# A fused attention and expert kernel: a ring of 27 results, expert shares on ScalarE, a dense layer in place

## What is computed

```python
xn = layernorm(x)
q, k, v = heads(xn @ Wq), heads(xn @ Wk), heads(xn @ Wv)          # 16 heads of 16
k_c, v_c = blocks_of_16(k) @ Wck, blocks_of_16(v) @ Wcv           # 32 blocks
logits_c = where(block_is_past, q @ k_c / 4, -1e9)
out_c = softmax(logits_c) @ v_c                                   # compressed blocks
top_idx = top_k(logits_c, 4)                                      # four blocks of each token
out_s = softmax(q @ k[tokens of top_idx] / 4) @ v[...]            # selected blocks
out_l = softmax(q @ k / 4 within the last 32 tokens) @ v          # local window
attn = (g0 * out_c + g1 * out_s + g2 * out_l) @ Wo
# expert layer: 4 heads, two sets of 64 keys, the best 8 of all pair sums
sx, sy = top_k(sim_x, 8), top_k(sim_y, 8)
scores, pk = top_k(sx[:, None] + sy[None, :], 8)
w = silu(xn . down_embed[idx]) * softmax(scores)
experts = sum(w * up_embed[idx])
mlp = (silu(xn @ Wg + bg) * (xn @ Wu + bu)) @ Wd + bd
out = x + attn + mlp + experts
```

## Time and profile before

| | |
|---|---|
| median of 3 executions | 1988.92 us (1987.8 to 1990.62) |
| the profiled execution | 1987.12 us, its span 1985.3 us |
| TensorE matmul busy | 1642.0 us, 83% |
| TensorE weight load busy | 1191.8 us, 60% |
| VectorE busy | 1366.6 us, 69% |
| ScalarE busy | 839.5 us, 42% |
| GpSimd busy | 918.3 us, 46% |
| granted TensorE clock, mean | 0.919 |
| stretch before the turns (0 to 262 us) | TensorE 208.21 us busy |
| stretch of the turns (262 to 1932 us) | TensorE 1396.57, VectorE 1252.15, ScalarE 731.27, GpSimd 819.15 us busy |
| stretch behind them (1932 to 1986 us) | TensorE 37.21 us busy |

### The profile page before, as it was taken

The page is one execution under the profiler, slowest core; times in us unless marked ns, Lnnn a source line. Parts: engine busy times, 40 slices in busy tenths (PEclk is TensorE's granted clock), DMA queues, the critical chain, the costliest instruction groups (busy, mean ns, idle before and its releaser), DMA issues. The chain is left out here.

```text
span 1985.3 us, 43216 instructions
## 1 busy us (share of the span) xinstructions
PE 1642.0 (83%) x14480; PEld 1191.8 (60%) x14480; DVE 1366.6 (69%) x4732; ACT 839.5 (42%) x1520; POOL 918.3 (46%) x741
## 2 busy tenths in 40 slices
PE   4999768888888888888888888888888888888867
PEld 3777636655555566666555655666565555566656
DVE  4344277777777777777777777777777777777742
ACT  0655234444344444444444444444444344444431
POOL 4533254455454554545555444454445545454420
PEclk7999878999899999998999899998999899999988
DMA  5455401111111101111111011111111111101017
GB/s 175 161 168 167 151 20 35 34 33 33 33 33 33 30 25 33 33 33 33 33 31 28 25 33 32 29 33 33 33 33 33 33 33 33 33 23 33 13 32 240
DMA packets 151611, 105.11 MB, mean 53 GB/s; under 512 B 63336, under 2 KB 145688, under 8 KB 151576
## 3 DMA queue, kind: packets, MB, share of 16 engines
q1 hardware_dynamic: 143128, 96.27, 16.5%
q10 hardware_dynamic: 8448, 8.39, 1.3%
HBM read 64.45 MB, written 40.16 MB: 53 GB/s over the span
## 5 line engine op out<-in xcount | busy, mean ns | idle before, releaser
L1076 POOL TENSOR_TENSOR cw<-cw,mw 128x1024 f32<-128x1024 f32 x96 | 226.7, 2362 | 368.0 <-DVE mw L1353 368.0
L1261 DVE TENSOR_REDUCE bmax<-q_bank 128x32 f32<-128x512 f32 (+3 forms) x512 | 227.0, 486 | 123.7 <-PE q_bank L1482 123.7
L1062 POOL TENSOR_TENSOR sumxy<-xy 128x1024 f32<-128x1024 f32 x128 | 240.8, 1903 | 0.0
L1137 ACT ACTIVATE pts<-k_bank 128x512 f32<-128x512 f32 (+2 forms) x384 | 185.0, 491 | 115.9 <-PE k_bank L1518 112.9
L1630 PE MATMUL y_bank<-wfd,hT 128*128 128x256 f32 x512 | 146.9, 412 | 76.5 <-DVE hT L1252 76.5
L1482 PE MATMUL q_bank<-ko,qo 96*128 96x512 bf16 (+3 forms) x512 | 144.6, 309 | 50.4 <-DVE bmax L1261 50.2
L1285 DVE TENSOR_REDUCE lmax<-q_bank 128x8 f32<-128x512 f32 x64 | 44.2, 691 | 196.9 <-PE q_bank L1504 196.9
L1047 POOL TENSOR_TENSOR shift_s<-unsel,smax_hi 128x496 bf16<-128x496 bf16 x32 | 32.6, 1017 | 310.3 <-DVE smax_hi L1300 310.3
L1464 PE MATMUL f_bank<-xt,wfg 128*128 128x128 f32 x1024 | 163.5, 289 | 0.0
L1464 PE MATMUL f_bank<-xt,wfu 128*128 128x128 f32 x1024 | 158.8, 277 | 0.0
L1630 PEld LDWEIGHTS y_bank<-wfd,hT 128*128 128x128 f32 x512 | 96.4, 204 | 100.0 <-DVE hT L1252 82.5
(11 more groups left out here) (231 smaller groups left out, 3751.2 us busy)
## 6 DMA issues: line engine op xcount, KB each, us to landing
qo<-s_qs SPq DMA_DIRECT2D x192, 64.0 KB, 2.2
ko<-s_ks SPq DMA_DIRECT2D x192, 64.0 KB, 2.2
s_qs<-parts SPq DMA_DIRECT2D x8, 768.0 KB, 3.8
s_ks<-parts SPq DMA_DIRECT2D x8, 768.0 KB, 6.2
s_v<-vo SPq DMA_DIRECT2D x8, 544.0 KB, 3.0
vv<-s_v SPq DMA_DIRECT2D x32, 136.0 KB, 2.3
xin<-in_L_attn_x_dram SPq DMA_DIRECT2D x8, 512.0 KB, 6.7
s_xt<-xT SPq DMA_DIRECT2D x8, 512.0 KB, 6.9
```

The lines of the kernel that those rows point to most:

```text
L1062: done("sum_done", g_.tensor_tensor(sumxy[:, h, :, :], xy[:, 0, h, 0:XK, None].broadcast_to([P, XK, KEYS]), xy[:, 1, h, None, :].broadcast ...
L1076: done("cw_sum", g_.tensor_tensor(cw[:, :], cw[:, :], mw[:, h % 2, :], ALU.add))
L1137: last = s.activation(pts[:, h, OFFS[j]:OFFS[j] + n], bank[:, 0:n], ACT.Exp)
L1261: last = v.tensor_reduce(bmax[:, i, h, 0:n], Q.bank(job)[:, o:o + n * BLK].rearrange("p (n j) -> p n j", j=BLK), AX.X, ALU.max)
```

## The change

**Ring K.** `pcT` is now the first result, `aug` and `co` share one bank as `augco`, and there are 27 results. On TensorE `block_shares` (the pcT transposes) stands between w0 and w1; `shifts_and_blocks` (aug and co) stands behind sim; `before_windows` (off) keeps its place among the rows of g0. Co no longer stands behind a0.

**Expert weights.** VectorE's two operations a head become one scalar_tensor_tensor, which also sums its row; ScalarE multiplies each row by 1/sum of the softmax (`share`); GpSimd adds the four rows. The reduction over cw goes: four sums, times erec, added. The last two operations of `last_expert` move to GpSimd.

**Dense layer.** tanh, gate and up work in hT itself; tanh of w0 and w1 in sw. `mlp_down` waits for u0 before its first part and for u1 before its third.

**Order.** On VectorE expert 3 moves ahead of the gate, `best_blocks` behind the experts, match_replace in two halves of eight into head 1's maxima, `best_keys` behind gate 1, `block_shares` ahead of the pair sums, and the shifts behind `normalize(t, 0)`. On GpSimd and ScalarE the order changes as shown.

```diff
-            k_jobs = ["aug", "pcT", "off", "a0", "co"]
+            k_jobs = ["pcT", "augco", "off", "a0"]
...
 # GpSimd
                     for h in range(PH):
                         done("sum_done", g_.tensor_tensor(sumxy[:, h, :, :], ...
-                        if h == 0:
+                        if h == 1:
+                            if now:
+                                silu_weights(now)
                             need(pool, "c8_done", t)
                             done("e8_in", g_.tensor_tensor(e8[:, :, :], ...
-                            if behind:
-                                silu_weights(behind)
+                def last_expert(t):
+                    need(pool, "csm_done", t)
+                    need(pool, "cw_sum", t)
+                    done("clast_sum", g_.tensor_tensor(clast[:, :], cw[:, EX - 1:EX], csum4[:, :], ALU.subtract))
+                    need(pool, "clast_sum", t)
+                    done("clast_done", g_.tensor_tensor(cw[:, EX - 1:EX], clast[:, :], four[:, :], ALU.add))
+                def weights(t, heads):
+                    for h in heads:
+                        need(pool, "ms_done", t, h + 1)
                         if h > 1:
                             need(pool, "cw_sum", t, h - 1)
+                        done("cw_sum", g_.tensor_tensor(cw[:, :], mw[:, 0, :] if h == 1 else cw[:, :], mw[:, h, :], ALU.add))
...
                 def step(t):
-                    weights(t)
+                    weights(t, (1,))
                     if n:
                         compressed(n)
-                    if n:
-                        candidates(n, behind=t)
+                    weights(t, (2, 3))
+                    last_expert(t)
+                    if n:
+                        selection(n, now=t)      # strike, pc_in
+                        candidates(n, now=t)
+                        result_in(t)
+                        block_shares(n)
+                        shifts(n)
...
 # ScalarE
+                def share(t, h):
+                    need(act, "mw_done", t, h + 1)
+                    done("ms_done", s.activation(mw[:, h, :], mw[:, h, :], ACT.Copy, scale=erec[:, h:h + 1]))
...
                 def step(t):
-                    tanh(t, "w0", tw[:, 0, :], "tw_done")
+                    tanh(t, "w0", sw[:, 0:512], "tw_done")
+                    block_shares(t)
                     expert(t, 0)
-                    tanh(t, "w1", tw[:, 1, :], "tw_done")
+                    tanh(t, "w1", sw[:, 512:EX], "tw_done")
                     expert(t, 1)
-                    shifts(t)
+                    share(t, 0)
+                    expert(t, 2)
                     if n:
                         key_scores(n)
+                    share(t, 1)
+                    shifts_and_blocks(t)
+                    expert(t, 3)
                     openings(t)              # off, a0, tanh of g0
+                    share(t, 2)
+                    share(t, 3)
                     head(t, 0)
                     head(t, 1)
-                    tanh(t, "g1", th[:, 1, :], "th_done")
+                    tanh(t, "g1", hidden(1), "th_done")
+                    if n:
+                        pc_exp(n)
                     head(t, 2)
                     if n:
                         e8_exp(n)
                     head(t, 3)
...
 # VectorE
                 def expert(t, h):
-                    cf.link(v.tensor_scalar(dst, sumxy[:, h, :, :]..., c8[:, h, 7:8], erec[:, h:h + 1], ALU.is_ge, ALU.mult))
+                    need(dve, "sum_done", t, h + 1)
                     need(dve, "ex_done", t, h + 1)
-                    done("mw_done", v.tensor_tensor(dst, dst, ex[:, h % 2, :], ALU.mult))
+                    done("mw_done", v.scalar_tensor_tensor(mw[:, h, :], sumxy[:, h, :, :]..., c8[:, h, 7:8],
+                                                           ex[:, h % 2, :], ALU.is_ge, ALU.mult, accum_out=csm[:, h:h + 1]))
...
                 def step(t):
                     expert(t, 2)
+                    expert(t, 3)
+                    expert_sum(t)
+                    if n:
+                        best_blocks(n)
                     gate(t, 0)
                     # maxima of head 0
                     up(t, 0)
-                    expert(t, 3)
+                    # selection(n, (0, 1)), maxima of head 1, selection(n, (2, 3))
                     gate(t, 1)
+                    # block_max(n, 2, 0), best_keys(n), block_max(n, 2, 1), block_max(n, 2, 2)
-                    last_expert(t)
                     up(t, 1)
+                    # unselected, best_pairs, maxima of head 3, block_shares, pair_sums, local_max(n, 0)
+                    normalize(t, 0)
+                    # local_max(n, 1), selected_max(n)
                     result(t)
-                    normalize(t, 0)
                     normalize(t, 1)
...
 # TensorE
                 def mlp_down(t, part):
                     if part == 0:
                         Y.wait_free(pe, t, "y")
-                        F.wait_read(pe, t, "u1")
+                    if part % 2 == 0:
+                        F.wait_read(pe, t, f"u{part // 2}")
...
                     token_rows(t, "w0", wdn, 0)
+                    block_shares(t)
                     token_rows(t, "w1", wdn, 512)
                     if n:
                         compressed(n)
-                    openings(t, 0)
-                    if n:
                         token_rows(n, "sim", wsim, 0)
                         loaded_by(pe, parts_in, N_PARTS, n)
-                    openings(t, 1)
+                    shifts_and_blocks(t)
                     up_rows(t, "g", 0, 0)
                     up_rows(t, "g", 0, 1)
-                    openings(t, 2)
+                    before_windows(t)
                     up_rows(t, "g", 0, 2)
                     head_shifts(t, 0)
                     up_rows(t, "g", 0, 3)
-                    openings(t, 3)
```

More of the change, by code:

```diff
@@ L1037, in compressed, with selection @@
                                                      block_no[:, :, None, :].broadcast_to([P, TT, HG, NB]), ALU.add))
-                def shifts(t):
+                def selection(t, now=None):
                     need(pool, "top_done", t)
@@ L1050, in shifts, with candidates @@
                         ALU.add))
[L1051 to L1055, removed]
+                def candidates(t, now=None):
                     need(pool, "xy_in", t)
@@ L1182, in openings @@
                 def openings(t):
-                    K.wait_full(act, t, "pcT")
-                    K.released("pcT", s.activation(pcT[:, :], K.bank("pcT")[:, :], ACT.Copy))
-                    expert(t, 2)
                     K.wait_full(act, t, "off")
@@ L1418, in step @@
                     up(t, 0)
-                    expert(t, 3)
                     if n:
+                        selection(n, (0, 1))
                         for part in range(3):
                             block_max(n, 1, part)
-                        best_keys(n)
+                        selection(n, (2, 3))
                     gate(t, 1)
@@ new lines, in before_windows @@
+                def before_windows(t):
+                    bank = K.bank("off")
+                    K.wait_free(pe, t, "off")
+                    K.wait_read(pe, t, "augco")
+                    mm(bank[96:128, 0:384], identb[:, 96:128], window_off[:, None, :].broadcast_to([P, 12, 32]),
+                       start=True, stop=True)
+                    for h in range(HG):
+                        for i in range(TT - 1):
+                            o = 32 * ((TT - 1) * h + i)
+                            tq = slice(P * (i + 1), P * (i + 1) + 32)
+                            mm(bank[96:128, o:o + 32], ko[0:SP3, t.half, h, P * i + 96:P * i + P], qo[0:SP3, t.half, h, tq],
+                               start=False, stop=False, skip_group_check=True)
+                            last = mm(bank[96:128, o:o + 32], headones[:, h, 0:32], shiftT[:, tq], start=False,
+                                      stop=True, skip_group_check=True)
+                    K.filled("off", last)
```

213 lines of the change are left out of this document (109 added, 104 removed).

## The result

The changed kernel takes 2008.71 us (median of 4 runs, 2007.99 to 2010.49); the kernel before, run beside it, 1989.18 (4 runs, 1987.8 to 1990.62). The ratio is 1.0099, 95% interval 1.0082 to 1.0117: slower by about 1%. The profiled execution took 2007.99 us with a span of 2006.1, so the span grew by 20.8.

The account below looks back on a forecast made before the run. A chain over several engines was taken to set each turn, 52.06 us before and 52.5 after. 31 x 0.44 = 13.6, less 4.8, made 1987.12 into 1995.9, plus 1.8 for the median: 1998 us, range 1945 to 2060.

Parts of the forecast that it names:

- tanh g0 (1) and (2): From w0 through ScalarE's row of work to off at 10.2, then 2.58 to tanh g0 at 12.75 us.
- strike done (3): GpSimd's cw sums of heads 2 and 3, 2.35 each, then four small operations including strike: done at 20.15 us.
- xy (4): VectorE's match_replace, head 1's maxima, gate 1 and best_keys, handing over to GpSimd's xy at 29.15 us.
- e8_in done (5): GpSimd's xy and cand, two sumxy, silu 2.35 and e8_in 0.24: done at 37.3 us.
- d3 (6): ScalarE's e8, then s30's exponentials: d3 starts at 38.05 us, after TensorE idles 5.6.
- Steps 7 and 8: d3 to the next w0, 11.72 us at full clock, plus 2.7 for half clock after the idle: 52.5 a turn.
- 31 x 0.44 = 13.6, less 4.8: Sum over turns: 31 turns each 0.44 us longer, the last turn 4.8 shorter, +8.8 us in all.
- The lead issues the same work: Work ahead of the first turn, given no term in the sum.
- rival 2: VectorE's fused operation walks its columns at half rate, some 2.15 us: 53.45 a turn, 2027 us; chance 0.12.
- Rival 1: TensorE's half clock after the d3 idle costs less: turns of 51.4 to 52.2, 1964 to 1989 us; chance 0.20.
- Rival 3: e8 comes early enough or hardly holds ScalarE: turns of 48 to 50, without d3 wait 44 to 45; chance 0.11.
- Rival 4: GpSimd and VectorE hold each other up and TensorE waits more at maxima: 54.5 a turn, 2060 us; chance 0.08.

Follow-up runs that it names:

- Runs 1 and 2: Changed kernel with GpSimd's e8_in behind the first sumxy, silu_weights behind the second: 1886.99 us; changed kernel with ScalarE's e8_exp behind head 3: 1879.8 us.
- run 4: Changed kernel with e8_in and then silu_weights both behind GpSimd's first sumxy, as in the kernel before: 1820.59 us, ratio 0.915.
- run 3: Changed kernel with the lead (work ahead of the first turn) put back into the order of the kernel before: 2007.36 us.
- run 8: Kernel of run 4 with the match_replace and unselected mask moved just ahead of local_max(n, 0), and best_keys ahead of gate 1: 1736.66 us, ratio 0.873.
- run 9: Kernel of run 8 with the expert shares (product with the reciprocal) moved from ScalarE back to VectorE: 1929.87 us, ratio 0.971.
- run 6: Kernel before with only mlp_down's waits changed, u0 before its first part and u1 before its third: 1875.72 us, ratio 0.943.

## Why the prediction was right or wrong

**The sign, the mechanism and the range held; the size was half.** Forecast were 1998 us, within 1945 to 2060, from a gain of two waits spent on a longer one at `d3`; measured 2008.71. Runs 1 and 2 show that mechanism by taking it away in two ways, and run 4 shows both halves of it (5.6 gained, 6.1 lost a turn). That the length of a turn came out within 0.1 (52.58 for 52.5) is in part luck: the chain up to d3 is 0.7 longer than forecast, what follows it on average 0.5 shorter, and 0.44 was a small difference of two long times.

**Steps 1 to 6, against the turn from 1013.49.** Each within 0.7 us:

| step | forecast t | measured t |
|---|---|---|
| tanh g0 (1) and (2) | 12.75 | 12.77 |
| strike done (3) | 20.15 | 20.2 |
| xy (4) | 29.15 | 29.7 |
| e8_in done (5) | 37.3 | 37.9 |
| d3 (6) | 38.05 | 38.7 |

TensorE idles 4.2 and not 5.6, because it came to `d3` at 34.5 and not at 32.4: it lost 4.0 at the maxima and 0.9 at `off`, where I counted 2.9 in all. That changes nothing in the sum, which runs over the chain.

**Steps 7 and 8.** d3 to the next w0 was 11.72 + 2.7 = 14.4 by the forecast. It was 14.6 in the turn shown (1052.21 to 1066.84) and 13.5 in the one ahead of it (999.97 to 1013.49), close to 11.72 and the half clock's 3.1 and 1.8; its mean of 2.2 is below my 2.7. A turn came to 52.58 for 52.5, that is 0.56 more than before where I had 0.44.

**The step that failed: "31 x 0.44 = 13.6, less 4.8", with "The lead issues the same work".** Of the 20.8 us the sum has 8.8.
- The removed wait stands in 31 of 32 turns: turn 0 has none, as nothing was normalized before it. The new one stands in turns 0 to 30. The sum gave the old wait back in turns 0 to 30 through the 0.44 and again in turn 31 through the -4.8: 32 times. Turn 0 measured +5.6 and not +0.44: 5.1 us missing. The count of times stood in the row that the forecast quoted.
- The count is not all of these 5.1. Turn 0 before is 1.9 shorter than the turns behind it (50.09 for 52.03), turn 0 after 3.1 longer (55.65 for 52.58), though its waits are those of the others (0.94, 1.34, 1.05, 0.45, 1.14, 4.20). What it has besides is half clock at its start: the slices of 1 us below (first of the kernel before, then of the changed one; the granted clock is the last figure but two) put its end at about 272.7 and 280.0, which is 1.7 us lost and 2.8. The forecast has no term for it; why it lasts longer after is open.
- w0 of turn 0 comes 5.2 later. Of this 1.0 is there ahead of the first unit's work already (GpSimd's first MEMSET of it at 236.20 for 235.26), unexplained by any edit. The rest follows from a lead in which best_blocks and match_replace stand ahead of the keys, so that xy starts at 260.29 and not 255.26, the 1.0 included. It does issue the same work, but in an order that hands it over later; and by run 3 the old order would not have helped, for the turn asks for `pc` earlier. Neither was looked at.
- The rest is small: 30 x 0.12 = 3.5 more in the middle turns, and -6.7 for -4.8 behind the last w0.

With the measured 5.1 of turn 0 and 5.2 of the lead the sum is 8.8 + 5.1 + 5.2 = 19.1, against 20.8 measured: so these two make up most of the miss.

```profile
272.00:273.00 1.00, 1.00 (x3) 0.52 (x2) 0.93 (x3) 0.05 (x1) 0.00 (x0) 0.68 0.00 0
```

```profile
280.00:281.00 1.00, 1.00 (x3) 0.28 (x2) 0.11 (x1) 0.77 (x1) 0.00 (x0) 0.98 0.00 0
```

**Edits costed one by one.** The fused operation: 1.28 and a read of 0.08 for the 1.25 taken, from VectorE's timeline:

```profile
1017.72 1.28 DVE L1394 SCALAR_TENSOR_TENSOR mw<-sumxy,c,ex 128x1024 f32<-128x1024 f32 x1
...
1024.69 1.61 DVE L1394 SCALAR_TENSOR_TENSOR mw<-sumxy,c,ex 128x1024 f32<-128x1024 f32 x1 [2.01 <-ACT ex L1175]
...
1049.58 1.66 DVE L1345 TENSOR_TENSOR cfac<-csum,gt 128x16 f32<-128x16 f32 x1
```

So rival 2 and its half rate fall: the Trainium skill's rule (Vector Engine (DVE) Microarchitecture Reference, "Points that are easy to get wrong") does not show here. Two float sources in SBUF with a row sum walk 1024 columns in 1.28, where the plain product takes 1.23. The 1.61 at 1024.69 begins 0.5 ahead of the end of GpSimd's first sum of cw (1022.87 and 2.35). ScalarE's shares: 1.04 apart as forecast (2.18 for two). Of VectorE's saving the forecast said that "it matters only on the chain below". For the part that moved to ScalarE that was too low a value: in the order of run 8 it is worth 6.3 us a turn, though this was measured there and not in the changed kernel itself.

**The rivals.** Rival 1 (clock cheaper): the loss of 1.8 to 3.1 lies on both sides of its 2.1, its mean of 2.2 just above, and the turns are not shorter. Rival 3 (e8 hidden) is what runs 1, 2 and 4 built, 46.4 to 48.7 a turn where it said 44 to 50; in the kernel as changed no slack absorbed the steps. Rival 4 was half there: TensorE waited 2.0 us more ahead of `d3` than counted (4.9 for 2.9), but off the chain.

## What to carry to other kernels

When a small operation is moved behind others on one engine, look at what is queued behind its consumer on the next: here 0.23 us of GpSimd work, moved behind a sum and silu_weights, held ScalarE and so TensorE for 4.2 us a turn, and the place of these two decided between 1% slower and 8.5% faster. Count the turns in which each wait stands, old and new, from its own row; the first and last turn are not the mean one, and a changed lead needs its own chain. And where VectorE and GpSimd both walk large tiles in SBUF, look at what an operation holds up beside its own duration: here moving four operations of 0.75 us to ScalarE was worth 6.3 us a turn, some 2.3 of it clock.

## What the runs showed of the hardware

- A VectorE operation on two float tiles in SBUF, or a tensor_scalar, that starts while GpSimd sums large tiles is held in these rows until GpSimd's operation ends: 3.00 for 1.28 and 2.71 for 0.75 (run 9). Each row is about 0.2 shorter than the rest of GpSimd's operation and its own time together. GpSimd is held likewise, 3.24 for 2.36. Even 16 columns are held: cfac, 0.17 in the lead of the kernel before (276.02, GpSimd idle), took 1.66 at 1049.58, until silu_weights ended (changed kernel).
- Four idles of about 1 us at the maxima and one at `off` in a turn leave the granted clock at 1.00 (run 4); idles of 4.2 bring it to 0.50, and it stays there for 3.7 to 6.1 us of renewed work in the two turns seen (changed kernel). In run 6, taking away a wait of 2.4 that stood apart from the one of 4.1 still raised the mean clock (0.93 to 0.95).
